# A gated-attention and mixture-of-experts kernel: large SBUF tensors allocated first, at exact multiples of 512 bytes

## The reference, cut to what is computed

```python
# layer 1: gated mLSTM attention, 16 heads of 64, causal over 512 rows
x = x + tanh(g_xattn) * mlstm(q=layernorm(x), k=ctx, v=ctx, gates Wi, bi, Wf, bf) * ln_scale
# layer 2: mixture of experts on h = layernorm(x)
probs = softmax(h @ router_w.T); the best 2 of 16 experts, their weights made to sum to 1
expert:  (silu(h @ gate_w[e]) * (h @ up_w[e])) @ down_w[e]        # 1024 -> 512 -> 1024
shared:  (silu(h @ sg) * (h @ su)) @ sd                           # 1024 -> 1024 -> 1024
x = x + tanh(g_ffn) * (shared + sum of the two experts' rows, weighted)
```

## Time and profile before

| what | value |
|---|---|
| three runs | 2937.93, 2942.51 and 2947.62 us (median 2942.51) |
| the profiled execution | 2930.05 us, of which the span is 2928.5 us |
| mean granted TensorE clock | 0.981 |
| TensorE matmuls | 95% busy, 17322 of them |
| TensorE weight loads | 78% busy |
| VectorE / ScalarE / GpSimd | 63% / 35% / 34% busy |
| DMA | 458.24 MB, 156 GB/s over the span |

### The profile page before, as it was taken

The page is one execution under the profiler, slowest core; times in us unless marked ns, Lnnn a source line. Parts: engine busy times, 40 slices in busy tenths (PEclk is TensorE's granted clock), DMA queues, the critical chain, the costliest instruction groups (busy, mean ns, idle before and its releaser), DMA issues.

```text
span 2928.5 us, 49266 instructions
## 1 busy us (share of the span) xinstructions
PE 2795.4 (95%) x17322; PEld 2293.6 (78%) x17323; DVE 1846.4 (63%) x2801; ACT 1015.4 (35%) x1948; POOL 993.3 (34%) x1147
## 2 busy tenths in 40 slices
PE   3799999999999977999999999999999999999999
PEld 2678778787877766888888888888888888888887
DVE  3787888788788855554455545545455457666666
ACT  4445444444544412333234324323333331111111
POOL 1343434443443433343344344334334311111111
PEclk7799999999999997999999999999999999999999
DMA  6555556555554534244444444444434326666665
GB/s 196 150 166 163 160 145 179 155 164 159 169 160 147 169 133 146 70 149 145 151 150 144 151 148 146 148 148 149 150 143 151 124 99 201 188 195 184 199 181 185
DMA packets 243470, 458.24 MB, mean 156 GB/s; under 512 B 99696, under 2 KB 131824, under 8 KB 240624
## 3 DMA queue, kind: packets, MB, share of 16 engines
q1 hardware_dynamic: 116976, 333.62, 33.9%
q0 software_dynamic: 34880, 73.10, 8.1%
q10 hardware_dynamic: 91488, 49.82, 6.5%
HBM read 358.96 MB, written 115.31 MB: 162 GB/s over the span
## 4 chain that ended last, share of the span: by engine, by line
PE 91%; DVE 4%; issue 2%; DMA 1%; ACT 1%; POOL 0%; SPq 0%; DVEq 0%; ACTq 0%; POOLq 0%
PE p_u L1624 40%; PE p_g L1610 10%; PE p_up L1610 10%; PE p_g L1021 6%; PE p_up L1021 6%; PE p_g L1036 3%; PE p_up L1036 3%; PE p_tr L958 2%; PE p_small L1107 2%; PE p_sc L1047 2%; PE p_u L1061 2%; PE p_u L1068 2%; PE p_sc L1597 1%; PE p_small L990 1%; PE p_u L1095 1%
## 5 line engine op out<-in xcount | busy, mean ns | idle before, releaser
L1624 PE MATMUL p_u<-w_hi,xt 128*128 128x512 f32 x3360 | 912.8, 394 | 2.8 <-DVE ctx_v L1506 2.8
L1624 PEld LDWEIGHTS p_u<-w_hi,xt 128*128 128x128 f32 x3360 | 627.6, 189 | 136.2 <-DVE ctx_v L1506 3.2
L1624 PE MATMUL p_u<-w_lo,xt 128*128 128x512 f32 x1680 | 525.8, 394 | 0.0
L1317 POOL DMA_INDIRECT xn<-mid_xn,idx_q x284 | 303.1, 1067 | 516.0 <-DVE lns L1489 422.0
L1624 PEld LDWEIGHTS p_u<-w_lo,xt 128*128 128x128 f32 x1680 | 315.4, 188 | 72.0 <-DVE w_lo L1455 5.1
L1478 DVE TENSOR_TENSOR ht<-p_sc,ht 128x512 fp32r<-128x512 f32 x74 | 51.0, 690 | 374.7 <-ACT ht L1393 374.7
L1455 DVE TENSOR_TENSOR w_lo<-stage,w_hi 128x1024 fp32r<-128x1024 f32 x200 | 230.2, 1219 | 81.1 <-ACT w_hi L1377 53.3
L1610 PE MATMUL p_g<-w_hi,ht 128*128 128x512 f32 x840 | 260.5, 392 | 1.8 <-DVE ht L1478 1.8
L1610 PE MATMUL p_up<-w_hi,ht 128*128 128x512 f32 x840 | 260.4, 391 | 0.0
L1438 ACT ACTIVATE th<-p_u 128x512 f32<-128x512 f32 x105 | 62.8, 598 | 554.7 <-PE p_u L1624 554.7
L1501 DVE SCALAR_TENSOR_TENSOR th<-th,p_u 128x512 f32<-128x512 f32 x105 | 72.2, 688 | 281.5 <-ACT th L1438 281.5
(11 more groups left out here) (220 smaller groups left out, 4707.3 us busy)
## 6 DMA issues: line engine op xcount, KB each, us to landing
mid_y<-uc SPq DMA_DIRECT2D x73, 512.0 KB, 2.6
stage<-mid_g_row SPq DMA_DIRECT2D x64, 512.0 KB, 5.7
stage<-in_eg SPq DMA_DIRECT2D x16, 2048.0 KB, 8.4
stage<-in_eu SPq DMA_DIRECT2D x16, 2048.0 KB, 14.8
stage<-in_ed SPq DMA_DIRECT2D x16, 2048.0 KB, 18.8
mid_y<-in_x SPq DMA_DIRECT2D x34, 512.0 KB
stage<-in_x SPq DMA_DIRECT2D x32, 512.0 KB
stage<-in_ctx_t ACTq DMA_DIRECT2D x32, 512.0 KB, 8.8
```

The costliest lines, as they stand in the source:

```text
L1317: nc.gpsimd.indirect_dma_start(out=xg_parts[:, n, :], out_offset=None, in_=xn_flat, in_offset=bass.IndirectOffsetOnAxis(ap=idx_q[:, n:n + ...
L1624: mm = nc.tensor.matmul(out[:, :], a[:, k, :], w[:, k, o:o + FE], start=(k == 0 and m == 0), stop=(k == KD - 1 and m == 2))
```

## The change

The allocation order in `build` is changed. A tensor `pad` of 384 bytes goes first, so that what follows starts at 16512 + 384 = 16896 = 33 x 512. Then come `stage`, `w_hi`, `w_lo`, `xt`, `ht`, `xn` and `x1`, then the small tensors that were first. `xt` and `ht`, which the mixing part allocated, are now allocated in `build` and handed over. Nothing is made larger or smaller. Besides, the functions of stage I (on GpSimd and on VectorE) and of stage O (on ScalarE and, in another form, on VectorE) return at once for any chunk but the last.

```diff
-    xt = sb("xt", [P, 2, KD, P], f32r)
-    ht = sb("ht", [P, 2, FE // P, P], f32r)
+    xt, ht = keep["xt"], keep["ht"]
...
         def stage_i(part, b, j):
+            if not is_last(b, j):
+                return
...
         def stage_o(part, b, j):
+            if not is_last(b, j):
+                return
...
-            if part < GUP // 2:
+            if is_last(b, j) and part < GUP // 2:
...
-        shapes = {"ident": [P, P], "iota_e": [P, NE], "hot_acc": [P, NE], "tgf": [P, 1],
-                  "eidx": [P, 2 * NCH], "rank": [P, 2 * NCH], "wts": [P, 2 * NCH]}
+        f32r, i32 = mybir.dt.float32r, mybir.dt.int32
+        keep = {"pad": ctx.enter_context(nc.sbuf_tensor("pad", [P, 96], f32))}
...
-        keep = {n: ctx.enter_context(nc.sbuf_tensor(n, s, f32)) for n, s in shapes.items()}
-        f32r, i32 = mybir.dt.float32r, mybir.dt.int32
         for n, s, dt in (("stage", [P, PIECES, D], f32), ("w_hi", [P, PIECES, D], f32r), ("w_lo", [P, PIECES, D], f32r),
-                         ("xn", [P, D], f32), ("x1", [P, 2, D], f32), ("idx", [P, 8], i32), ("quarter", [P, 8], i32), ("idx_q", [P, 8], i32), ("starts_i", [P, 2, NE + 1], i32)):
+                         ("xt", [P, 2, KD, P], f32r), ("ht", [P, 2, FE // P, P], f32r), ("xn", [P, D], f32), ("x1", [P, 2, D], f32),
+                         ("ident", [P, P], f32), ("iota_e", [P, NE], f32), ("hot_acc", [P, NE], f32), ("tgf", [P, 1], f32),
+                         ("eidx", [P, 2 * NCH], f32), ("rank", [P, 2 * NCH], f32), ("wts", [P, 2 * NCH], f32),
+                         ("idx", [P, 8], i32), ("quarter", [P, 8], i32), ("idx_q", [P, 8], i32), ("starts_i", [P, 2, NE + 1], i32)):
             keep[n] = ctx.enter_context(nc.sbuf_tensor(n, s, dt))
```

## The result

The changed kernel takes 2921.51 us (median of 4 runs, 2918.98 to 2923.20) against 2942.86 us (4 runs, 2937.93 to 2947.62): the ratio is 0.9927, 95% interval 0.9908 to 0.9946. It is faster, by 0.5 to 0.9%.

What follows compares the result with a forecast made beforehand. The prediction took TensorE's 9864 wide matmuls at 229.0 ns, 77% of the span, as the bound. Its terms, 0 + 0 + 0 - 0.3 us, on the median 2942.51 gave 2942 us, range 2924 to 2958 us.

Steps and rivals of the forecast that it cites:

- (b): Wide matmuls' moving operand: 15.7 ns each above streaming time, at most 155 us to gain from operands' place; taken as 0.
- R2: Wide matmuls get faster with both operands on multiples of 512: 2903 us (saved crossing) or 2787 us (whole excess); chance 0.08.
- R3: Small gains by DMA and start-up in the first 130 us: 7 us and as much again, 2928 us; chance 0.12.
- R4: Slower: wide matmuls' load and stream collide at agreeing low bits, 3001 us; milder in mixing part, 2945 to 2957; chance 0.12.
- (a): TensorE's weight loads, seen on the transposes: equal cost at 32 and 480, hidden with 40 ns to spare; 0 us.
- (c): VectorE and ScalarE: operands' place shows nothing beyond 10 ns on 512 elements; 0, with +-2 us.
- (d): DMA transfers, on the chain for 29 us, mostly in the first 130 us: gain 0.3 to 7 us, taken as 0.3.

Runs made afterwards that it cites:

- e11: Changed kernel with the moving operands w_hi and w_lo at 96 past a multiple of 512, the rest at 0: 2967.84 us in one run.
- e1: Changed kernel with only the moving operands w_hi and w_lo back at 32 past a multiple of 512: 2965.37 us, ratio 1.0104 to the kernel before.
- e2: Changed kernel with only the stationary operands xt and ht back at 480 past a multiple of 512: 2966.55 us, ratio 1.0106 to the kernel before.
- e6: Changed kernel with w_hi, w_lo, xt and ht all at 32 past a multiple of 512: 2924.50 us, ratio 0.9952 to the kernel before.
- e4: Changed kernel's order without the pad, every large tensor at its place mod 512 of before the change: 2935.99 us, ratio 0.9998 to the kernel before.
- e3: Changed kernel with only stage, xn and x1 back at 32 past a multiple of 512: 2922.84 us, ratio 0.9953 to the kernel before.
- e17: Changed kernel without the pad, all large tensors at 128 past a multiple of 512: 2923.06 us, ratio 0.9953 to the kernel before.
- e13: Changed kernel with the low half of xt alone moved to 32 past a multiple of 512: 2945.09 us in one run.
- e15: Changed kernel with the moving operands w_hi and w_lo at 160 past a multiple of 512, the rest at 0: 2978.78 us in one run.
- e16: Changed kernel with xt and ht 8 bytes behind the place that agrees with w_hi and w_lo (488 against 480): 2946.22 us in one run.
- e12: Changed kernel with xt and ht 16 bytes behind the place that agrees with w_hi and w_lo (496 against 480): 2966.80 us in one run.
- e18: Changed kernel with the moving operands w_hi and w_lo at 448 past a multiple of 512, xt and ht at 0: 2967.14 us in one run.

## Why the prediction was wrong

**The step that failed is (b), the moving operand, "I take 0 us".** It had the right place, the 9864 wide matmuls, and the right doubt: the trace had one single combination of low bits, and "it doesn't exclude that the 15.7 ns come from it". It then took 0 because rows with one operand's place varied were equal. But those rows couldn't bear on it. VectorE's rows are another engine, and the transposes of the earlier trace rows stream 128 columns of plain float32, one every 109 ns. The change moved `ident` and `stage` from 96 bytes apart to 0 (mod 512), and within a group the transposes of `stage` start 108.8 ns apart on average before and 108.6 ns after: 96 costs the wide matmuls 3% (e11), and these, if `stage` is the stationary one as the prediction had it, nothing that shows. The term was 2.22 ns a matmul, of which the expert part's 7560 count: 16.8 us by the pace, 13.4 us measured in the two profiled executions. The other 2304, in the mixing part, brought nothing. There the prediction had read TensorE as busy for about 97% off one stretch of the earlier trace rows; over the whole part it is 89% (1023.5 of 1147.95 us).

**R2 had the direction, and neither its mechanism nor its sizes.** It priced a crossing of multiples of 512 in each operand by itself (39 us) or all of the excess (155 us). e1 and e2 have each one operand back on its place of before and are slower than the kernel that has both; in e6 the weights' rows cross as many multiples of 512 as before, and it is as fast as the changed kernel.

**R3 was not what happened.** The first 100 us hold 40.0 us of matmuls for 39.7. The chain's first row out of SBUF, 5.38 us before, takes 4.21 us here, and GpSimd's first work on `var` starts at 97.9 us for 100.6, but in the other kernels that start lies between 98.5 and 101.7 us wherever `stage` is, so no gain there is shown.

**R4 had the pair of operands, with the sign turned.** It feared starts that agree in the low bits. Agreement (a distance of 0 or 256) is the best of the twelve distances measured, and disagreement the usual dear case. The kernel before had, by accident, the second best: 64. That is why undoing half of the change costs 1.5% of the changed kernel's time (e1, e2: 44 and 45 us) though undoing all of it costs 0.5 to 0.7% (e4, and the change itself). Its threshold, a load longer than the 229 ns, isn't what decides: the loads of this line keep 188 to 189 ns on average in every kernel here.

**(a) held, as far as it went**: the transposes of L963 take 139 ns for the load with `stage` at 0 and 141 with `th` at 352 (before 141 and 140):

```profile
L963 PEld LDWEIGHTS p_tr<-ident,stage x256: 137/139/231, 12.1 to 1005.0; 128*128 128x128 f32 x128
...
L963 PEld LDWEIGHTS p_tr<-ident,th x128: 138/141/231, 136.9 to 1145.7; 128*128 128x128 f32 x128
```

**(c) held for the place**: with `stage`, `xn` and `x1` at 32 the time is the same (e3). L1494's transposes changed by 3%, but not with their operands' place (e3, e1), and VectorE isn't what ends the tile.

**(d) had the right direction and was hidden**, as argued: the load of the up weights lands 0.7 us earlier with `stage` at 0 and again later in e3, at the same time of the kernel. The 0.3 us that it put on the sum can't be told from scatter by any run. By the rule on starts off a multiple of 256 bytes (the Trainium skill, page "DMA: Bandwidth & Descriptors", section "How a descriptor splits into AXI transactions") the transfers had to get a little shorter, and the trace agrees in direction: 6.3 for 6.5% in the small packets' queue, 14.1 for 14.8 us to the landing of the up weights. The skill's page words the rule for bytes that are fetched, and the up weights are written into `stage`, so its reason isn't shown by that second number.

**The early returns and the counts held**: 49266 instructions, the same groups.

**The size of the gain.** First 21.3 us (ratio 0.9927, 0.9908 to 0.9946), but 13 to 16 us (0.9953, 0.9952, 0.9953) in later sets of runs for e3, e6 and e17, which have the same pace. Their times, 2922.8, 2924.5 and 2923.1 us, are close to the changed kernel's 2921.5; what differs is the kernel before, 2942.9 us in the first set and 2935.6 to 2940.5 in the later ones. The expert part alone accounts for 13.4 us between the two profiled executions (14.4 us against e4's), and the pace for up to 17. For the rest of the first difference I have no cause but the scatter of the kernel before.

**What stays open.** That the two reads of TensorE, load and stream, meet in SBUF is my guess at why the distance counts, and not shown; e13 fits it in part (the largest loss falls where the shifted half is loaded) but no run separated the two reads. That the effect needs a load for each matmul isn't tested either: no kernel here streams twice over one load. Why 64 is cheap and -64 isn't, and why a mixture costs more than its parts (e13), is not settled. Nor is what sets the 226.7 ns that are left at distance 0. The 215.7 ns that the Trainium skill gives for 512 columns back to back (page "TensorE: Matmul & The Clock Gate", section "Wait — 56ns, not 53.3ns?") was reached at none of the distances measured. And the count overstates the cost at the dear distances: from its first to its last matmul the expert part takes 1804.4 us in e1 and 1762.7 in the changed kernel, 41.7 us more where 7560 x 6.67 ns makes 50.4, and the mixing part isn't longer at all (it ends at 1152.9 us for 1154.5). Lined up as above, e1 loses 28.7 us in the routed tiles (5.7 ns a matmul) and 15.2 us in the shared ones, and wins 2.6 us in the second tile, where in e1 the clock is already back at 1.00. In the mixing part the wide matmuls are dearer too (L1026: 233.1 for 229.0 ns between two starts after 150 us, intervals of 300 ns and more left out), and yet it doesn't last longer; what hides that was not traced, nor why the routed tiles lose less than the shared ones.

## What to carry to other kernels

In a float32r stream of wide matmuls that TensorE runs without a pause, with a load for each, look at the start of the moving operand less that of the stationary operand. Here 0 (and 256, in one run) was best, and most others cost 3% of the pace. The tensors needn't lie at a round address, they must lie alike; a small tensor put in or taken out between them moved this kernel by 1.5% (e1, e2 against the changed kernel), and by 2% at the worst distance (e15, one run), with no instruction changed. The whole gain over the kernel before was 0.5 to 0.7%, since its distance happened to be a cheap one. And where a trace holds one combination of something, equal rows for its parts on other streams say nothing about the pair: that belongs in the range.

## What the runs showed of the hardware that was not expected

- TensorE's distance between wide float32r matmuls at a granted clock of 1.00 takes values from 226.7 to 234.3 ns (from the recorded starts) by the distance of the two operands' starts, with the lowest at distances 0 and 256, and with the loads' recorded duration unchanged. Transposes of 128 columns don't show it.
- 8 bytes of distance already cost 4 ns (e16), 16 bytes the full 6.7 (e12).
- VectorE's transposes of 128x1024 (L1494) take 2201 ns in the changed kernel, e3 and e17, 2276 before, 2298 in e1, and up to 2362 (e18). They didn't follow the place of their input or of their output mod 512; what they do follow was not tested.
